# First bias rows by a closed-form variance, the second gain moved behind the transposes, weight splitting shared with ScalarE, and gate constants moved to set-up

## The reference, cut to what matters

```python
def ln(x, g, eps=1e-05):
    mean = x.mean(axis=-1, keepdims=True)
    var = ((x - mean) ** 2).mean(axis=-1, keepdims=True)
    return (x - mean) * jax.lax.rsqrt(var + eps) * g

def rel_pos_bias(n, w0, b0, g0, w1, b1, g1, w2, b2, dtype):
    pos = jnp.arange(-n + 1, n, dtype=dtype)[:, None]
    h = jax.nn.silu(ln(pos @ w0 + b0, g0))
    h = jax.nn.silu(ln(h @ w1 + b1, g1))
    h = h @ w2 + b2
    ...

xn = ln(x, g_norm)
q = (xn @ Wq) ...            # 16 heads of 64
kv = xn @ Wkv                # one key and one value head for all
q = l2norm(q) * q_scale ; k = l2norm(k) * k_scale      # a null key stands ahead of the keys
sim = q k^T * 8 + bias ; causal mask, row mask ; softmax ; times v
x = x + ln(out @ Wout, g_out)
```

## Time and profile before

| what | value |
|---|---|
| median of 3 runs | 1698.6 us (1697.67 to 1698.99) |
| the profiled execution | 1698.69 us |
| its span, first to last instruction | 1696.8 us |
| mean granted TensorE clock | 0.963 |
| busy: PE, DVE, ACT, POOL | 86%, 84%, 71%, 46% |

### The profile page before, as it was taken

How to read it: one execution, slowest core, us unless ns; L and a number is a source line. 1 busy time by engine, 2 the same in 40 slices (tenths; PEclk the granted TensorE clock), 3 DMA queues, 4 the chain that set the end, 5 groups by cost and what they waited for, 6 DMA issues and landing times.

```text
span 1696.8 us, 44687 instructions
## 1 busy us (share of the span) xinstructions
PE 1458.7 (86%) x15551; PEld 1070.0 (63%) x15551; DVE 1420.2 (84%) x3579; ACT 1210.8 (71%) x3073; POOL 776.7 (46%) x1551
## 2 busy tenths in 40 slices
PE   2567677788899999997788888999999989999998
PEld 1345555566677777775566666777777756666665
DVE  3567777879898999986788888899999979888887
ACT  1466767877898989987788888999999923333332
POOL 6666676644444434446665332322222256642322
PEclk8578989999999999998999999999999999999999
DMA  4002121111221222202222111212223101000000
GB/s 141 22 20 63 39 63 51 52 63 64 76 76 48 86 95 92 85 14 52 63 76 70 51 70 68 81 64 85 88 101 115 38 1 37 9 1 1 14 14 26
DMA packets 50625, 96.58 MB, mean 57 GB/s; under 512 B 3476, under 2 KB 27236, under 8 KB 50404
## 3 DMA queue, kind: packets, MB, share of 16 engines
q1 hardware_dynamic: 47988, 92.65, 16.5%
q10 hardware_dynamic: 2416, 1.07, 0.3%
HBM read 91.54 MB, written 2.17 MB: 55 GB/s over the span
## 4 chain that ended last, share of the span: by engine, by line
PE 49%; DVE 20%; ACT 12%; issue 10%; POOL 3%; DVEq 0%; ACTq 0%; POOLq 0%
PE tp L1621 8%; DVE p_lo L1200 6%; DVE biased L1099 6%; ACT p_hi L829 5%; PE sc L1301 4%; PE sc L1303 4%; PE sc L1302 4%; PE sc L1499 4%; PE sc L1500 3%; ACT q_b L755 3%; PE op L1301 2%; ACT probs L734 2%; PE tp L1301 2%; PE tp L1303 2%; PE tp L1302 2%
## 5 line engine op out<-in xcount | busy, mean ns | idle before, releaser
L1200 DVE TENSOR_TENSOR p_lo<-tp,p_hi 128x512 f16<-128x512 f32 (+3 forms) x768 | 411.9, 554 | 118.9 <-ACT p_hi L829 112.4
L734 ACT ACTIVATE probs<-biased,neg_max 128x256 f32<-128x256 f32 (+7 forms) x512 | 395.6, 773 | 19.4 <-DVE neg_max L1099 18.4
L1621 PE MATMUL tp<-ident,probs 128*128 128x128 f32 x2304 | 393.8, 280 | 17.8 <-DVE p_lo L1200 13.8
L829 ACT ACTIVATE p_hi<-tp 128x512 f16<-128x512 f32 (+3 forms) x768 | 366.7, 491 | 29.7 <-PE tp L1621 19.8
L1301 PE MATMUL op<-v_s,p_hi 128*128 128x64 f16 x2304 | 286.7, 195 | 54.5 <-DVE p_lo L1200 31.3
L1499 PE MATMUL sc<-k_a,q_a 128*128 128x512 f16 (+3 forms) x768 | 256.1, 334 | 85.5 <-DVE neg_max L1099 78.1
L1621 PEld LDWEIGHTS tp<-ident,probs 128*128 128x128 f32 x2304 | 271.3, 143 | 54.3 <-issue 34.8
L1303 PE MATMUL op<-v_s,p_lo 128*128 128x64 f16 x2304 | 285.5, 194 | 0.0
L1302 PE MATMUL op<-v_s,p_hi 128*128 128x64 f16 x2304 | 285.5, 194 | 0.0
L1301 PEld LDWEIGHTS op<-v_s,p_hi 128*128 128x128 f16 x2304 | 217.4, 99 | 83.8 <-DVE p_lo L1200 52.5
L1500 PE MATMUL sc<-k_b,q_b 128*128 128x512 f16 (+3 forms) x768 | 244.4, 332 | 0.0
(11 more groups left out here) (291 smaller groups left out, 3598.5 us busy)
## 6 DMA issues: line engine op xcount, KB each, us to landing
bias<-rel_table SPq DMA_DIRECT2D x4, 2048.0 KB, 8.5
bias<-in_fside_16xSxS SPq DMA_DIRECT2D x4, 2048.0 KB, 8.3
...
```

The costliest lines, as they stand in the source:

```text
L734: ac.activation(probs[:, i % 2, 0:w], biased[:, i % 2, 0:w], ACT.Exp, bias=neg_max[:, u % 2, i % HU:i % HU + 1], scale=-1.0, accum_out=row ...
L829: ac.activation(p_hi[:, gi % 4, 0:nb * P], tp[gi % 2][:, 0:nb * P], ACT.Copy)\
L1200: ve.tensor_tensor(p_lo[:, gi % 4, 0:nb * P], tp[gi % 2][:, 0:nb * P], p_hi[:, gi % 4, 0:nb * P], ALU.subtract).then_inc(s["p_lo"], 1)
L1621: last = te.transpose(tp[gi % 2][:, jj * P:(jj + 1) * P], probs[:, n % 2, (j0 + jj) * P:(j0 + jj + 1) * P], ident[:, :])
```

## The change

- **Layer 1 of the table.** The variance of `w0 * pos + b0` is a polynomial of `pos`: the variance of `w0`, that of `b0`, and their cross term. `table_vectors` computes these three once, then the variance of all 1024 positions as a tile of 128x8 (`rel_v`); POOL takes all roots in one instruction (`rel_root`). Both vectors are centred, halved and multiplied by `g0` in advance. A round's layer 1 is then two `table_line`, two tanh on ACT with the row's scale `rel_rs`, and `table_active`. Its root is multiplied back behind `w1` (`table_mixed`).
- **Layer 2.** `g1` is no longer multiplied in on DVE. The normalised rows are transposed first, ACT's tanh takes them from PSUM with `g1` as scale (`table_tanh2`), DVE's `table_active2` reads them from PSUM and writes `rht`, and `g1 / 2` is multiplied into `w2` once (`table_gains`).
- **Weights.** For `Wkv` and the first layer's `Wq`, ACT scales and casts in large instructions (`weight_half`), POOL only subtracts (`low_half`).
- **Null key.** `null_keys` is cut into `null_product` and `null_sum`, at the steps -14, -12 and -10.
- **Gates.** `gate_prep` and `gate_const` move from the steps 119 and 123 to -8 and -6, with PE's part.
- **Loads.** On SP `Wq` goes ahead of `w1`, the masks wait for `Wq`, the gates' small loads go ahead of the rest of `x`. On ACT the broadcast of `g1` is gone, a column of `g1` is added behind `g_norm`.

```diff
-        FILL = {-18: (STATS, 0), -17: (SCALE, 0), -15: (ACTIVE, 0), -14: (MIX, 0),
-                -10: (SCALE, 1), -9: (ACTIVE, 1), -8: (OUT, 1)}
-        ROUND = {0: (STATS, 0, 0), 1: (STATS, 0, 1), 4: (SCALE, 0, 0), 5: (GAIN, 0, 0), 6: (ACTIVE, 0, 0),
-                 7: (TURN, 0, 0), 8: (MIX, 0, 0), 11: (MIX, 0, 1), 13: (SCALE, 1, 0), 14: (GAIN, 1, 0),
-                 18: (ACTIVE, 1, 0), 19: (TURN, 1, 0), 20: (OUT, 1, 0)}
-        ROOTS = {2: 0, 12: 1}
...
+        ROUND = {0: (LINE, 0), 1: (LINE, 1), 6: (ACTIVE, 0), 7: (TURN, 0), 8: (MIX, 0), 11: (MIX, 1),
+                 14: (SCALE, 0), 19: (TURN2, 0), 20: (OUT, 0)}
+        TANH_AT, ROOT_AT = 2, 12
...
             load_job(sp, 0)
+            load_job(sp, 1)
             sp.dma_start(w1_sb[:, :, :], a["L0_cond_w1"].rearrange("(k p) n -> p k n", p=P)).then_inc(s_in["w1"], 16)
...
-            load_job(sp, 1)
+            sp.wait_ge(s_stage[1], 16)
...
+            def rel_root():
+                pool.wait_ge(setup["var"], 1)
+                link(gp.tensor_scalar(rel_v[:, :], rel_v[:, :], r_mv[:, 1, 1:2], EPS, ALU.add, ALU.max))
+                gp.tensor_tensor(rel_rs[:, :], rel_v[:, :], mhalf[:, 0:TILES], ALU.pow).then_inc(setup["root"], 1)
...
+            def low_half(n):
+                jn, hi, lo, at_, w, gain, gc = pieces[n]
+                pool.wait_ge(setup["half"], 2 if jn == 0 else 4)
+                gp.tensor_tensor(lo, stage[:, jn % 2, at_:at_ + w], hi, ALU.subtract).then_inc(job_done, 1)
...
             pool.wait_ge(s_in["gain"], 16)
-            split_to(job_end[0])
-            SPLITS = {-17: 2, -16: 2, -15: 2, -13: 1, -9: 1}
+            gp.tensor_scalar(g_ws[:, :], g_in[0][:, :], WS, 1.0, ALU.mult, ALU.mult).then_inc(setup["vec"], 1)
...
+            def weight_half(jn, kc, per):
+
+                act.wait_ge(s_stage[jn % 2], stage_value[jn])
+                src = stage[:, jn % 2, kc * per:(kc + 1) * per]
+                dst = (wkv if jn == 0 else wq)[0][:, 0, kc, :]
+                ac.activation(src, src, ACT.Copy, scale=g_ws[:, kc:kc + 1]).then_inc(act_chain, 1)
+                act.wait_ge(act_chain, 1 + jn * KC + kc)
+                ac.activation(dst, src, ACT.Copy).then_inc(setup["half"], 1)
...
+            def table_vectors():
+
+                dve.wait_ge(s_in["rel"], 4 * 16)
+                dve.wait_ge(setup["rel"], 1)
+                for i in range(2):
+                    last = ve.bn_stats(r_st[:, i, :], rvec[:, i, :])
+                link(last)
+                for i in range(2):
+                    last = ve.bn_aggr(r_mv[:, i, :], r_st[:, i, :])
+                link(last)
+                for i in range(2):
+                    last = ve.tensor_scalar(rvec[:, i, :], rvec[:, i, :], r_mv[:, i, 0:1], 0.5, ALU.subtract, ALU.mult)
+                last = ve.tensor_scalar(r_mv[:, 1, 1:2], r_mv[:, 1, 1:2], EPS, None, ALU.add)
+                link(last)
+                link(ve.tensor_tensor_reduce(out=junk, in0=rvec[:, 0, :], in1=rvec[:, 1, :], scale=8.0 / D, scalar=0.0,
+                                             op0=ALU.mult, op1=ALU.add, accum_out=cross[:, :]))
+                link(ve.tensor_scalar(rel_v[:, :], rel_f[:, :], r_mv[:, 0, 1:2], cross[:, 0:1], ALU.mult, ALU.add))
+                ve.tensor_tensor(rel_v[:, :], rel_v[:, :], rel_f[:, :], ALU.mult).then_inc(setup["var"], 1)
+                link(ve.tensor_tensor(rvec[:, 0:2, :], rvec[:, 0:2, :],
+                                      rvec[:, 2, :].unsqueeze(1).to_broadcast([P, 2, D]), ALU.mult))
...
+            def table_active2(r, bank):
+
+                dve.wait_ge(setup["tanh2"], 2 * r + 2)
+                ve.scalar_tensor_tensor(rht.rearrange("p c k n -> p (c k n)"), re.rearrange("p k n -> p (k n)"), 1.0,
+                                        bank, ALU.add, ALU.mult).then_inc(setup["h2"], 1)
...
-                if part == OUT:
-                    table_out(0, sc[1][0:H, 0:2 * P])
-                    null_keys()
+                if n == -14:
+                    table_active(0)
+                    null_product(0)
+                    null_sum(0)
...
+                if n == -12:
+                    null_product(1)
+                if n == -10:
+                    table_scale(0)
+                    null_sum(1)
+                    null_columns(0)
...
+                if n == -8:
+                    table_out(0, sc[1][0:H, 0:2 * P])
+                    gate_prep(op)
+                if n == -6:
+                    gate_const(aux)
```

More of the change, by code:

```diff
@@ L184, in model @@
         r_rs = sb("r_rs", [P, 2])
+        rel_v = sb("rel_v", [P, TILES])
+        rel_rs = sb("rel_rs", [P, TILES])
+        cross = sb("cross", [P, 1])
+        g1_c = sb("g1_c", [P, KC])
+        g_ws = sb("g_ws", [P, KC])
         rh = moe_w[:, 0:512].rearrange("p (k n) -> p k n", k=2)
@@ L260, in model @@
         setup = sems("setup", """mhalf ident rel place ones penalty big nss nrinv
-                    mt cb lg lgh stats rstd z tanh h pt t mm mid pad tab""")
+                    mt cb lg lgh half vec var root u tanh h pt t mm mid stats rstd n tanh2 h2
+                    pad tab""")
         s = sems("attn", """scores bias biased probs
@@ L273, in model @@
         pool_chain = sem("pool_chain")
+        act_chain = sem("act_chain")
         table_in = sem("table_in")
@@ L276, in model @@
         s_stage = [sem(f"stage_in{i}") for i in range(2)]
-        s_in = {name: sem("in_" + name) for name in ("x", "x1", "rel", "gain", "w1", "w2", "head", "late", "mask", "moe")}
+        s_in = {name: sem("in_" + name) for name in ("x", "x1", "rel", "gain", "g1", "w1", "w2", "head", "late", "mask", "moe")}
         def bcast(ap, n):
@@ L434, in _ @@
                     .then_inc(s_in["mask"], 16)
-            for b in range(B):
-                sp.dma_start(x_sb[:, b, 1:TILES, :], x_in[:, b, 1:TILES, :]).then_inc(s_in["x1"], 16)
-            load_job(sp, 2)
             sp.dma_start(cond_n, a["cond_64"]).then_inc(s_in["moe"], 16)
@@ L441, in _ @@
                 sp.dma_start(wg_n[:, i, :], a[pre + "wg"]).then_inc(s_in["moe"], 16)
+            for b in range(B):
+                sp.dma_start(x_sb[:, b, 1:TILES, :], x_in[:, b, 1:TILES, :]).then_inc(s_in["x1"], 16)
+            load_job(sp, 2)
             write_table(sp, 0)
@@ new lines, in table_line, with table_active @@
+            def table_line(r, i):
+                if r > 0 and i == 0:
+                    dve.wait_ge(setup["pt"], 2 * r)
+                k_ = TILES - 2 - 2 * r + i
+                ve.scalar_tensor_tensor(rh[:, i, :], rvec[:, 0, :], rel_f[:, k_:k_ + 1], rvec[:, 1, :],
+                                        ALU.mult, ALU.add).then_inc(setup["u"], 1)
+            def table_active(r):
+                dve.wait_ge(setup["tanh"], 2 * r + 2)
+                ve.scalar_tensor_tensor(rh, re, 1.0, rh, ALU.add, ALU.mult).then_inc(setup["h"], 1)
@@ L882, in table_stats, with table_mixed @@
+            def table_mixed(r, i, src):
+                dve.wait_ge(setup["mm"], 3 * r + 1 + i)
+                if r == 0 and i == 0:
+                    dve.wait_ge(setup["root"], 1)
+                k_ = TILES - 2 - 2 * r + i
+                ve.scalar_tensor_tensor(rh[:, i, :], src, rel_rs[:, k_:k_ + 1], rvec[:, 3, :], ALU.mult, ALU.add)\
+                    .then_inc(setup["mid"], 1)
+                dve.wait_ge(setup["mid"], 2 * r + 1 + i)
                 last = ve.bn_stats(r_st[:, i, :], rh[:, i, :])
@@ L1183, in small @@
                             .then_inc(s["ot_lo"], 1)
-                    r, step_ = in_round(n, ROUND)
-                    if r and step_[0] == MIX:
-                        table_mixed(r, step_[2], second[:, 0:D])
-                    if r and step_[0] == OUT:
+                    r, step_, at_ = in_round(n)
+                    if step_ == MIX:
+                        table_mixed(r, at_, second[:, 0:D])
+                    if step_ == TURN2:
+                        table_active2(r, second)
+                    if step_ == OUT:
                         table_out(r, second[0:H, 0:2 * P])
-                    if n == PREP[0]:
-                        gate_prep(second)
-                    if n == PREP[1]:
-                        gate_const(second)
                 now = plan.at(n)
```

248 lines of the change are left out of this document (129 added, 119 removed).

## The result

| | before | changed |
|---|---|---|
| median of 4 runs | 1698.8 us (1697.67 to 1699.02) | 1670.8 us (1669.04 to 1671.55) |
| ratio, 95% interval | | 0.9835 (0.9818 to 0.9852) |
| span of the profiled execution | 1696.8 us | 1668.7 us |
| mean granted TensorE clock | 0.963 | 0.973 |

The change gives 28 us. The prediction said 13.2 and a range down to 1679.0: the direction was right, and the size forecast was less than half of what came. (A slip of the description: N, the number of steps, is 512, two layers of 8 tiles of 32 steps; the expert layers follow.)

The account below looks back on a forecast made before the run. PE carries half the chain, but the start and speed of the first 96 steps count, with POOL setting the set-up's pace from 51.38 to 71. 6.2 + 2.0 + 4.3 + 0.7 = 13.2 gave 1685.5 us, range 1679.0 to 1693.0.

Parts of the forecast that it names:

- Set-up, 6.2: Before step 0: the null term comes at 49.4 instead of 55.61, 6.2 us earlier, and the first row at about 50.
- the column: Set-up load of `g_norm` on which POOL waits: issued one load earlier, taken to land at 12.0, bounds 10.3 to 14.9.
- POOL's closed gap: POOL in the set-up: its 4.69 us wait for the new `q_ss` behind the masks would be gone.
- the null term: POOL's set-up result that the first bias row needs: at 49.4 where it came at 55.61, 6.2 us earlier.
- The gates' price in the set-up: `gate_prep` moved ahead of `k_b` in the set-up: fits while POOL is in the masks, 0, bounds 0 to 2 us.
- Round 1, 2.0: First of the rounds in steps 0 to 95: 2.0 us gained, POOL's root of 1.0 counting in full.
- Rounds 2 and 3, 4.3: Later rounds of steps 0 to 95: half of the removed chain pieces' 8.6 us taken as gain, 4.3 us.
- The chain's 8.6 us: Rounds 2 and 3, 133.54 to 247.96: 18 pieces on the chain that go, 8.6 us together, as upper bound.
- The gates, 0.7: Four pieces of `gate_prep` and one of `gate_const` leave the chain, 1.0 us together; 0.7 taken as gain.
- rival 3: Slower by the clock: PE stays at the lower level up to 200 us, +4.5 us, 1703.1; chance 0.05.
- rival 1: Column late or masks hold `gate_prep`, and the steps refill: 5 to 6 us gained, 1693; chance 0.20.
- The faster side: Whole kernel measurably faster, beyond the 3.4 us that a measurement can tell from no change: chance 0.88.

Follow-up runs that it names:

- a1: The changed kernel with the gates' constants back at steps 119 and 123, all else as changed: 1676.4 us, 0.9868 of the kernel before.

## Why the prediction was half right

The direction was right, the size not: 28 us came, 13.2 were forecast and 19.6 was the most that the range allowed. Two steps failed above all, the pricing of rounds 2 and 3 and that of the gates.

- **Set-up, 6.2: right in size** (5.7), with the column (12.08 for 12.0), the masks and POOL's closed gap where the working had them. That the size fits is partly luck: I took it from the null term, which moved by 7.3, while the row stands behind `q_ss`. (`gate_prep` has nine instructions on DVE, not 13.) The gates' price in the set-up, taken as 0, is 2.7 us at the first row by a1 and nothing a few steps on.
- **Round 1, 2.0: wrong,** 5.3. I counted POOL's root as 1.0 and the rest as a small extra. In the profiles the work brought back 1.1, the root with DVE's wait 2.2 (of which 1.6 may be scatter), the tight chain 0.8, and 1.2 stays open.
- **Rounds 2 and 3, 4.3: this step failed most,** 12.3. "A piece on the chain bounds the gain from above" was the error, and halving it doubled the error. The chain's 8.6 us held the removed instructions and not the waits that they caused: a wait for POOL's root shows as work of whoever ended it. The restored work alone brought back 6.9, the root 2.5, and the whole is 12.3. The sum also had nothing for the clock, which went from 0.86 and 0.88 to 1.00 in the steps 32 to 48 and 64 to 80; its share is open but for the estimate above.
- **The gates, 0.7: wrong,** 5.8. I priced the pieces of DVE on the chain (nine short ones of `gate_prep`, 1.2 us, where I had read four) and didn't look at the engine that handed over the bank: the row with 2.69 us of PE's idle time was in the trace, and the 0.42 behind it too. I had searched the clock for a loss (rival 3) and had given its gain no term in the sum, only a mention in the range. Of the 5.6 us that came back in a1, 2.6 were the clock's.
- **Rivals.** The masks did hold `gate_prep` (rival 1) without its consequence, the column wasn't late, nothing was refilled, and the clock didn't stay down (rival 3).

The faster side with 0.88 held; the range didn't, since its lower end took the chain's pieces in full as a bound.
